# Attention layers of a graph network: where the three parts of an item's sums are added together

## The reference

```
feat = (h @ W).reshape(N, 4, 64)
e    = leaky_relu(el[src] + er[dst], 0.2)      # el, er: one number per node and head
a    = softmax of e over the edges that end in the same node
out[dst] = sum over edges of a * feat[src]
```

## Time and profile before

| | us |
|---|---|
| median of three runs | 4631.3 |
| the profiled execution, its own time | 4628.58 |
| its span, first to last instruction | 4626.8 |
| layer g0a, first mask to last step | 2298.9 to 2809.3 |
| layer g1a | 2905.8 to 3394.5 |
| layer g3a | 4102.2 to 4612.4 |

### The profile page before, as it was taken

The page is one execution under the profiler, slowest core; times in us unless marked ns, Lnnn a source line. Parts: engine busy times, 40 slices in busy tenths (PEclk is TensorE's granted clock), DMA queues, the critical chain, the costliest instruction groups (busy, mean ns, idle before and its releaser), DMA issues. The chain is left out here.

```text
span 4626.8 us, 74673 instructions
## 1 busy us (share of the span) xinstructions
PE 2702.0 (58%) x26874; PEld 2350.3 (51%) x26874; DVE 3322.3 (72%) x5484; ACT 2361.5 (51%) x4268; POOL 1566.3 (34%) x1226
## 2 busy tenths in 40 slices
PE   2222222048610466553388884799857998648897
PEld 2112111024410333332288884799846888548887
DVE  4998666134310677777688897899978999688897
ACT  3222222000100233232488894899958999578897
POOL 0877888876667778782000000000000000100000
PEclk7555555579855566666699997899978999879999
DMA  6223222266200222221111110212102121012111
GB/s 263 33 33 48 32 32 8 0 137 167 61 17 15 47 46 46 47 46 17 38 44 60 47 57 5 74 42 64 55 7 72 44 62 57 8 41 70 44 56 58
DMA packets 330179, 242.46 MB, mean 52 GB/s; under 512 B 86728, under 2 KB 318410, under 8 KB 328906
## 3 DMA queue, kind: packets, MB, share of 16 engines
q1 hardware_dynamic: 246474, 188.80, 13.9%
q0 software_dynamic: 82304, 29.95, 6.7%
q10 hardware_dynamic: 1152, 20.58, 1.1%
HBM read 211.56 MB, written 27.68 MB: 52 GB/s over the span
## 5 line engine op out<-in xcount | busy, mean ns | idle before, releaser
L484 POOL DMA_INDIRECT table<-adj_value,adj_cell x392 | 641.3, 1636 | 197.9 <-issue 190.0
L985 POOL DMA_INDIRECT l_row<-node_rows,l_rec x416 | 506.7, 1218 | 133.0 <-issue 126.5
L1443 PE MATMUL g0a_ps<-g_parts,g0a_pos 128*128 128x195 bf16 x2500 | 437.3, 250 | 120.5 <-DVE g0a_side L1555 119.8
L1443 PE MATMUL g3a_ps<-g_parts,g3a_pos 128*128 128x195 bf16 x2500 | 435.2, 249 | 122.6 <-DVE g3a_side L1555 103.7
L1443 PE MATMUL g2a_ps<-g_parts,g2a_pos 128*128 128x195 bf16 x2500 | 431.0, 248 | 101.2 <-DVE g2a_side L1555 101.1
L1443 PE MATMUL g1a_ps<-g_parts,g1a_pos 128*128 128x195 bf16 x2500 | 431.1, 248 | 100.4 <-DVE g1a_side L1555 99.6
L999 PE MATMUL l_ps<-l_value,l_hot 128*128 128x260 f32 x832 | 365.7, 607 | 203.6 <-DVE l_acc L1142 116.9
L704 DVE TENSOR_SCALAR_CACHE_REDUCE adj_same<-adj_rows,adj_key 128x1792 bf16<-128x1792 f32 (+1 forms) x392 | 448.7, 1209 | 19.2 <-DMA adj_rows<-key_rows 9.4
L539 PE MATMUL adj_ps<-adj_pair,adj_same 128*128 128x2 bf16 x2940 | 133.5, 165 | 553.0 <-DVE adj_same L704 550.3
L1470 ACT ACTIVATE g3a_side<-g3a_er,g_elb 128x512 f16<-128x512 f32 (+1 forms) x700 | 407.9, 664 | 65.4 <-PE g3a_ps L1445 61.2
L1470 ACT ACTIVATE g0a_side<-g0a_er,g_elb 128x512 f16<-128x512 f32 (+1 forms) x700 | 407.9, 664 | 64.9 <-PE g0a_ps L1445 61.5
(11 more groups left out here) (382 smaller groups left out, 6191.6 us busy)
## 6 DMA issues: line engine op xcount, KB each, us to landing
gcn_cols<-table SPq DMA_DIRECT2D x24, 1600.0 KB, 9.5
adj_rows<-key_rows SPq DMA_DIRECT2D x28, 896.0 KB, 4.7
table<-zeros ACTq DMA_DIRECT2D x8, 2512.5 KB, 27.1
g0a_cols<-table SPq DMA_DIRECT2D x8, 1024.0 KB, 5.4
g1a_cols<-table SPq DMA_DIRECT2D x8, 1024.0 KB, 5.4
g2a_cols<-table SPq DMA_DIRECT2D x8, 1024.0 KB, 5.5
g3a_cols<-table SPq DMA_DIRECT2D x8, 1024.0 KB, 5.5
l_row<-node_rows,l_rec POOLq DMA_INDIRECT x416, 2.6
```

Source lines behind the costliest of these rows:

```text
L484: pool.indirect_dma_start(out=table.rearrange("(w o) -> w o", o=1), out_offset=bass.IndirectOffsetOnAxis(cell[:, u, k:k + 1], 0), in_=valu ...
L985: pool.indirect_dma_start(out=row[:, u, k, :], out_offset=None, in_=node_rows, in_offset=bass.IndirectOffsetOnAxis(rec[:, j, 0:1].bitcast( ...
L1443: pe.matmul(bank[:, 0:HW], pos[:, slot, b - b0, j * P:(j + 1) * P], parts[:, b, 0, k, :], start=(b == 0), stop=False, skip_group_check=True)
```

## The change

ScalarE writes `taken` sorted by part, and in two copies, one per side, in place of one. `evacuated` counts by two. GpSimd, which had been idle, waits for an item's two copies, issues a DMA within SBUF that adds the low part onto the middle one, waits for it, issues a second that adds the middle part onto the high one, and signals `all_added`. VectorE's `add_middle` and `add_low` go. The other steps move: `scale` of item n-2 stands at q = 0, `both` at q = 1, `invert` at q = 2, `divide` at q = 3 and `add` at q = 4. `scale` waits for `all_added`.

```diff
-        taken = s.sb("taken", [P, 2, GB, 2 * HW], F32)
+        taken = s.sb("taken", [P, 2, 3, GB, 2, DW], F32)
...
+        low_added, all_added = s.pool_dma_sem("low_added"), s.pool_dma_sem("all_added")
...
-                pe.wait_ge(evacuated, n + 1)
+                pe.wait_ge(evacuated, 2 * n + 2)
...
+        @block.gpsimd
+        def _(pool):
+            for n in range(ITEMS):
+
+                part = [taken[:, n % 2, c, 0:WIDTHS[n // H]].rearrange("p j s f -> p (j s f)") for c in range(3)]
+                pool.wait_ge(evacuated, 4 + 2 * (n + 1))
+                pool.dma_start(part[1], part[2], accum_op=ALU.add).then_inc(low_added, 16)
+                pool.wait_ge(low_added, 16 * (n + 1))
+                pool.dma_start(part[0], part[1], accum_op=ALU.add).then_inc(all_added, 16)
...
-                act.copy(taken[:, n % 2, 0:nblk, :], ps[:, GB * (n % 2):GB * (n % 2) + nblk, 0:2 * HW]).then_inc(evacuated, 1)
-            act.sem_inc(evacuated, 2)
+                banks = ps[:, GB * (n % 2):GB * (n % 2) + nblk, :]
+                act.copy(taken[:, n % 2, :, 0:nblk, 0, :].rearrange("p c j f -> p j c f"),
+                         banks[:, :, 0:HW].rearrange("p j (c f) -> p j c f", c=3)).then_inc(evacuated, 1)
+                act.copy(taken[:, n % 2, :, 0:nblk, 1, :].rearrange("p c j f -> p j c f"),
+                         banks[:, :, HW:2 * HW].rearrange("p j (c f) -> p j c f", c=3)).then_inc(evacuated, 1)
+            act.sem_inc(evacuated, 4)
...
-            def add_middle(n):
-                dve.wait_ge(evacuated, 2 + n + 1)
-                step.add(dve.tensor_tensor(third(n, 0), third(n, 0), third(n, 1), ALU.add))
-
-            def add_low(n):
-                dve.wait_ge(step.sem, step.n)
-                step.add(dve.tensor_tensor(third(n, 0), third(n, 0), third(n, 2), ALU.add))
...
             def scale(n):
-                dve.wait_ge(step.sem, step.n)
+                dve.wait_ge(all_added, 16 * (n + 1))
...
-                    if n >= 1:
-                        {4: add_middle, 5: add_low, 6: scale}.get(q, lambda n: None)(n - 1)
                     if n >= 2:
-                        {0: both, 1: invert, 2: divide, 3: add}.get(q, lambda n: None)(n - 2)
-            for part in (both, invert, divide, add):
-                part(ITEMS - 2)
-            for part in (add_middle, add_low, scale, both, invert, divide, add):
-                part(ITEMS - 1)
+                        {0: scale, 1: both, 2: invert, 3: divide, 4: add}.get(q, lambda n: None)(n - 2)
+            for n in (ITEMS - 2, ITEMS - 1):
+                for part in (scale, both, invert, divide, add):
+                    part(n)
```

More of the change, by code:

```diff
@@ L1484, in link @@
                 dve.wait_ge(step.sem, step.n)
-            def third(n, c):
-                return taken[:, n % 2, 0:WIDTHS[n // H], :].rearrange("p j (s c f) -> p (j s) c f", s=2, c=3)[:, :, c, :]
             def places(n):
@@ L1492, in places, with summed @@
                 return slice(FIRST[i], FIRST[i + 1]), slice(k * D, (k + 1) * D), k, WIDTHS[i]
-            def add_middle(n):
-                dve.wait_ge(evacuated, 2 + n + 1)
-                step.add(dve.tensor_tensor(third(n, 0), third(n, 0), third(n, 1), ALU.add))
-            def add_low(n):
-                dve.wait_ge(step.sem, step.n)
-                step.add(dve.tensor_tensor(third(n, 0), third(n, 0), third(n, 2), ALU.add))
+            def summed(n):
+                return taken[:, n % 2, 0, 0:WIDTHS[n // H], :, :]
             def scale(n):
                 rows, at, k, nblk = places(n)
-                dve.wait_ge(step.sem, step.n)
-                step.add(dve.tensor_tensor(third(n, 0), third(n, 0), spread(t["vs"][:, k, rows, :].rearrange("p b s -> p (b s)"), 2 * nblk, DW), ALU.mult))
+                dve.wait_ge(all_added, 16 * (n + 1))
+                parts_sum = summed(n).rearrange("p j s f -> p (j s) f")
+                step.add(dve.tensor_tensor(parts_sum, parts_sum, spread(t["vs"][:, k, rows, :].rearrange("p b s -> p (b s)"), 2 * nblk, DW), ALU.mult))
             def both(n):
@@ L1509, in both @@
                 dve.wait_ge(step.sem, step.n)
-                sides = taken[:, n % 2, 0:nblk, :].rearrange("p j (s f) -> p j s f", s=2)
-                step.add(dve.tensor_tensor(total[:, 0:nblk, :], sides[:, :, 0, 0:DW], sides[:, :, 1, 0:DW], ALU.add))
+                sides = summed(n)
+                step.add(dve.tensor_tensor(total[:, 0:nblk, :], sides[:, :, 0, :], sides[:, :, 1, :], ALU.add))
             def invert(n):
```

## The result

The changed kernel took 4652.7 us (median of seven runs, 4646.1 to 4660.7) and the kernel before, beside it, 4620.2 (median of seven, 4612.5 to 4639.1). The ratio is 1.0062, with a 95% interval of 1.0046 to 1.0078: by it the change costs 29 us, 21 to 36 (the medians lie 32.5 apart). Forecast were 38 us (4667), from 4648 to 4683. The profiled executions span 4650.9 and 4626.8 us, 24.1 apart.

What follows compares the result with a forecast made beforehand. The prediction took a loop of waits through TensorE, ScalarE's masks and VectorE's q = 0 step as the bound, not VectorE's fullness. Terms 0 + 12 + 3 + 0 + 23 = +38 us on 4628.6 gave 4667 us, from 4648 to 4683.

Steps and rivals of the forecast that it cites:

- two additions off VectorE: Steady items: VectorE sheds 78 us of work, but the additions are not on the chain, so 0 us.
- `scale` at q = 0: Wide loop: `scale` replaces the shorter `both`, adding 0.20 us to each of 60 items, 12 us; narrow items 0.
- second copy: ScalarE: covered in wide items, inside the narrow loop at 0.06 us for 44 items, 3 us in all.
- waits for transfers inside a layer: Steady items: the two transfers' 7.0 us fit the cover of 12.0 (wide) and 9.3 (narrow), so VectorE waits 0.
- ends of the layers: After each layer's last copy nothing covers the transfers: `scale` starts 5.8 us later, four times, 23 us.
- rival B: TensorE's loop turns in g0a and g3a: six stalls vanish (-44 us, chance 0.12) or six more come (+44, 0.08).
- The chain: Waits setting an item's period: the wide loop runs through TensorE, ScalarE's masks and VectorE's q = 0 step, never the additions.
- L: Time of the two adding transfers together, hand-overs included: 7.0 us, ends 5.4 and 8.8, up to 12.5 if issuing is stretched.
- rival C: GpSimd's issuing is stretched beside VectorE: transfers take 11.8 us, narrow items pay 44 us, 4711 us in all; chance 0.08.
- the rule of its summary: GpSimd's descriptor generation is starved while VectorE is in a fast mode; by it the transfers would outlast their cover.
- Rival D: Adding within SBUF is slow, 7 us a transfer: waits in narrow and wide items, +218 us, 4847 us; chance 0.07.

Runs made afterwards that it cites:

- no additions: The kernel before with `add_middle` and `add_low` left out, so only the high part enters the result: 4614.6 us, ratio 0.9970.
- the slot alone: The kernel before with its steps one slot later (`scale` at q = 0), additions still by VectorE, one copy, no transfer: 4624.9 us, ratio 1.0001.
- kernels without the lag: VectorE's `negative` no longer one unit late: kernel before 4466.0 us; changed kernel, last item by VectorE, 4466.7; kernel before, both additions left out, 4456.5.

## Why the prediction was right

The direction, the size and the mechanism held. Its terms, over four layers:

| step | predicted | measured |
|---|---|---|
| two additions off VectorE | 0 | 0 (no additions: same periods) |
| `scale` at q = 0 | +12 | +8 (the slot alone: 2.2 and 2.0 a layer; its wide items by themselves: 10) |
| second copy | +3 | +3 (0.9 and 0.6 a layer) |
| waits for transfers inside a layer | 0 | 0 (one of 0.35 us in g0a, one of 0.47 in g3a) |
| ends of the layers | +23 | +22 (5.3 and 5.5 a layer) |
| sum | +38 | +33 |
| TensorE's stalls | 0 (rival B: -44 or +44) | -9.5 in this pair of profiles |

**What bounds it.** Busy 19.03 of 20 (93% over eight whole items) did not mean bound. The chain was right, and the kernel without additions settled it: 1.2 us an item taken off the busiest engine moved nothing. The kernels without the lag are the other half of the proof: once the loop is shorter, the same 1.2 us is worth 0.5 an item.

**The slot.** I priced 60 items at 0.20. The items became 0.18 longer (18.81 against 18.63), and there are 56 of them, not 60: `scale` stands at q = 0 from a layer's third item on, which leaves 14 wide ones. That gives 10. The layers say 8, since other items differ too: in g2a the narrow ones are 0.07 shorter with the steps moved (14.84 instead of 14.91), and a layer's first item varies by some 0.2 from profile to profile.

**The transfers.** L was predicted as 7.0 us, from rows of other transfers; it is 6.5 for narrow items and some 7.1 for wide ones (an estimate: 0.3 to the first issue, 3.55 from issue to issue, 3.3 to the landing). Issuing took 863 ns, steady beside VectorE's masks (at most 1053 in any layer), so rival C has fallen. Of the Trainium skill's two rules the exemption for two-input instructions (SBUF — State Buffer, Who interferes with whom) is the one that the trace bears out, and the rule of its summary did not bite here. Rival D has fallen at medians of 3.0 to 3.9 us a transfer. What I did not see is that a column load stretches the chain to 10.5 us. In wide items it fitted under the 12 us by luck of the slot, and in narrow ones just (the waits of 0.35 and 0.47 us are at such a turn); my statement that the ends of L are 5.4 and 8.8 was wrong for these items.

**Rival B** happened in part. It is the difference between the terms' 33 us and the span's 24 (another 0.8 lies between layers). As the stalls of g0a come and go by chance, it was luck that these did not move the sum further.

## What to carry to other kernels

A ring of engines has a period set by its longest loop, not by its fullest engine. Before work is taken off an engine, look for that work in the chain of a steady period; if it isn't there, the relief is worth nothing until the loop is shorter, and moving another step into a slot of the loop makes things worse. A transfer that is hidden in the steady state is bare at each end of a stage, so the last item is better done by the old way.

## What was not expected of the hardware

- Adding transfers within SBUF land after 3.0 us (195 KB) and 3.3 us (260 KB), 0.86 of it issuing; in g3a the median of the larger ones was 3.9. Beside column loads of 1 MB one takes 5.1 to the next issue.
- A stall at the turn of TensorE's loop costs 7 to 10 us an item in g3a (up to 12 where a transfer is late too), in every profile of a kernel with loops, and in g0a it comes 0, 1 or 3 times. TensorE pauses 4 to 7 us in it, and the rest is the lower granted clock behind the pause and a second, shorter pause.
- A wait of 2.8 us on VectorE became 4.1 us of a pair of items, with TensorE's granted clock at 0.76 in the stretch of 5 us around it and 0.90 in the next.
